# Cross-attention front end: q projected in transposed form, keys stacked four heads at a time

## The reference

```python
def w8a8_linear(x, w, b):                      # int8-like product
    qx, sx = dyn_quant(x)                      # one scale sx per token (row of x)
    qw, sw = quant_weight(w)                   # one scale sw per output channel
    return einsum('bnc,oc->bno', qx, qw) * (sx * sw[:, 0]) + b

q = w8a8_linear(layernorm(x), wq, bq)          # (32, 112, 512), as 16 heads of 32
k = ctx @ wk.T + bk                            # (32, 375, 512)
v = ctx @ wv.T + bv
attn = softmax(q k^T / sqrt(32) + mask)
x1 = x + w8a8_linear(attn v, wo, bo)
out = x1 + mixture_of_experts(layernorm(x1))   # 8 experts, top 2 of them per token
```

## Time and profile before

| | before |
|---|---|
| median of 3 runs | 1605.53 us |
| the profiled execution | 1609.71 us, its span 1608.0 us |
| TensorE busy | 1494.6 us (93%) |
| VectorE, ScalarE, GpSimd busy | 897.5, 884.0, 660.6 us |
| mean granted TensorE clock | 0.965 of full speed |
| DMA, HBM traffic | 281.09 MB moved; 83568 of 220124 packets under 512 B |

### The profile page before, as it was taken

How to read it: one execution, slowest core, us unless ns; L and a number is a source line. 1 busy time by engine, 2 the same in 40 slices (tenths; PEclk the granted TensorE clock), 3 DMA queues, 4 the chain that set the end, 5 groups by cost and what they waited for, 6 DMA issues and landing times. The chain is left out here.

```text
span 1608.0 us, 40123 instructions
## 1 busy us (share of the span) xinstructions
PE 1494.6 (93%) x11594; PEld 1317.6 (82%) x11595; DVE 897.5 (56%) x2365; ACT 884.0 (55%) x2097; POOL 660.6 (41%) x671
## 2 busy tenths in 40 slices
PE   2899999999999999999999999984399999999896
PEld 2788888888888888888888888873299999999895
DVE  6557666766676667666766676654632222222221
ACT  2467667677777776777677767761033333333232
POOL 4233334333443234323432343323555555656453
PEclk9999999999999999999999999985599999999998
DMA  5567777677767776777677767654537776666643
GB/s 173 145 170 196 209 200 197 179 228 205 194 178 226 202 196 179 225 205 196 178 225 201 200 179 222 185 142 141 160 68 186 182 175 134 148 154 125 160 77 48
DMA packets 220124, 281.09 MB, mean 175 GB/s; under 512 B 83568, under 2 KB 164976, under 8 KB 220080
## 3 DMA queue, kind: packets, MB, share of 16 engines
q1 hardware_dynamic: 203952, 247.24, 54.3%
q0 software_dynamic: 16128, 33.30, 11.6%
HBM read 118.31 MB, written 66.17 MB: 115 GB/s over the span
## 5 line engine op out<-in xcount | busy, mean ns | idle before, releaser
L464 DVE CUSTOM_DVE_ANT_0 probs<-score,neg_mask 112x375 f32<-112x375 f32 x512 | 279.7, 546 | 254.8 <-PE score L555 251.5
L392 ACT ACTIVATE probs<-probs,neg_max 112x375 f32<-112x375 f32 x512 | 312.3, 610 | 197.2 <-DVE neg_max L464 191.7
L563 PE MATMUL turn<-ident,probs 112*125 112x112 f32 x1536 | 264.8, 282 | 2.8 <-ACT probs L392 2.5
L385 ACT ACTIVATE probs_t<-turn 125x336 f32<-125x336 f32 x512 | 226.0, 441 | 71.6 <-PE turn L563 70.6
L563 PEld LDWEIGHTS turn<-ident,probs 112*125 112x125 f32 x1536 | 227.2, 190 | 36.4 <-issue 14.4
L555 PE MATMUL score<-k_stack,q_stack 96*112 96x376 f32 x512 | 209.4, 409 | 8.5 <-DMA q_stack<-q_lo 6.2
L591 PE MATMUL proj<-ctx_hi,wk_hi 128*128 128x376 f32 x512 | 176.0, 344 | 1.9 <-PEq L29 1.1
L591 PE MATMUL proj<-ctx_lo,wk_hi 128*128 128x376 f32 x512 | 172.0, 336 | 0.0
L591 PE MATMUL proj<-ctx_hi,wk_lo 128*128 128x376 f32 x512 | 171.7, 335 | 0.0
L1032 DVE TENSOR_TENSOR a_lo<-a_ps,a_hi 128x384 fp32r<-128x384 f32 x63 | 35.1, 557 | 243.7 <-ACT a_hi L1007 243.7
L596 PE MATMUL proj<-wv_hi,ctx_hi 128*125 128x512 f32 x384 | 151.8, 395 | 0.0
(11 more groups left out here) (198 smaller groups left out, 3393.9 us busy)
## 6 DMA issues: line engine op xcount, KB each, us to landing
k_stack<-k_hi SPq DMA_DIRECT2D x512, 94.0 KB, 2.2
k_stack<-k_lo SPq DMA_DIRECT2D x256, 94.0 KB, 2.2
ctx_stage<-ctx_t SPq DMA_DIRECT2D x32, 750.0 KB, 5.0
q_stack<-q_hi SPq DMA_DIRECT2D x256, 56.0 KB, 2.0
w_raw<-gate_up_t SPq DMA_DIRECT2D x32, 352.0 KB, 3.1
gate_up_dram_hi<-w_hi SPq DMA_DIRECT2D x32, 352.0 KB, 4.8
gate_up_dram_lo<-w_raw SPq DMA_DIRECT2D x32, 352.0 KB, 5.2
gate_up_hi<-gate_up_dram_hi SPq DMA_DIRECT2D x16, 704.0 KB, 4.9
```

The costliest lines, as they stand in the source:

```text
L385: act.activation(probs_t[:, h % RING_T, :, :], turn[h % 2][0:LC, 0:LT * N].rearrange("p (l n) -> p l n", l=LT), ACT.Copy).then_inc(turned_ ...
L392: act.activation(probs[:, h % DS, :], probs[:, h % DS, :], ACT.Exp, bias=neg_max[:, par % 2, h:h + 1], scale=-1.0, accum_out=total[:, par ...
L464: dve.tensor_tensor_reduce(probs[:, h % DS, :], score[h % 2][0:N, 0:L], neg_mask[:, p, :], 1.0, BIG, ALU.add, ALU.min, neg_max[:, p, h:h + ...
L563: mm = pe.transpose(turn[h % 2][0:LC, l * N:(l + 1) * N], probs[:, h % DS, l * LC:(l + 1) * LC], W["ident"][0:N, 0:N])
```

## The change

1. Order of channels. The host permutes the output channels of `wq` and `wk` (and both biases) so that head h = 4i + g has its 32 channels on partitions 32i to 32i+31 of group g. The four heads 4i to 4i+3 are then one block of 32 partitions.
2. Keys. `stack_keys(i)` moves four heads by 3 transfers (12 a pass, 24 before), each row contiguous (4 x 376 values). Quarter 3 of the batch is issued at the start of its own pass, quarters 0 to 2 in the pass before. Each needs all four groups of k_lo (before: two), and waits for the scores of the four heads that it overwrites. TensorE waits at heads 0, 4, 8 and 12; ScalarE at h = 3 waits for all four quarters before the first `k_hi` (before: at h = 3 and 7 for one half each).
3. q transposed. At h = 7 sixteen products (bf16, weights 128x128 from `wq_int`, 112 moving columns of `x_int_t`) give q with channels on partitions. The four float32 transposes at h = 9 and their wait for GpSimd go.
4. Scales. The channel scale is now a column, the token scale must be a row: `x_scale` is stored to DRAM at the end of the pass that makes it (112 elements of 4 bytes), fetched as a row spread over 128 partitions in the next pass, and GpSimd multiplies row and column to `q_scale` (128x448), ahead of the bias. VectorE's `q_t` (h = 8) waits for it.
5. q to its place. `q_hi` and `q_lo` (both now from `q_t` in SBUF) are stored together to DRAM by one transfer; SyncE waits until it has landed (`q_kept`), then fetches by 3 transfers. Before: 12 transfers from SBUF to SBUF.
6. SyncE's order: the loads of expert weights stand behind the stores of x1 and h2, x, and the scale row. `q_dram` is issued between quarter 0 and quarter 1 of the keys.
7. `prepare_weights`: no row of channel scales for q (four small activations, eight product records and one copy fewer). VectorE gets 14 semaphore increments ahead of its loop (`LOOP_OFFSET`).

The core of the diff:

```diff
@@ prepare_weights
-            for i, (_, _, row) in enumerate(pairs):
-                act.wait_ge(row_made, i + 1)
-                act.activation(row[0:N, :], ps[0:N, :], ACT.Copy, scale=-inv_sqrt_d if i == 0 else 1.0).then_inc(row_out, 1)
+            act.wait_ge(row_made, 1)
+            act.activation(W["wo_row"][0:N, :], ps[0:N, :], ACT.Copy).then_inc(row_out, 1)
...
+            dve.tensor_scalar(W["wq_col"][:, :], scale[:, 0, :], -inv_sqrt_d, None, ALU.mult).then_inc(bias_done, 1)
@@ attention, SyncE
+            def stack_keys(i):
+
+                rows = slice(QUARTER * i, QUARTER * i + QUARTER)
+                for r, src in ((0, k_hi), (1, k_lo), (2, k_hi)):
+                    sp.dma_start(k_st[QUARTER * r:QUARTER * r + QUARTER, G4 * i:G4 * i + G4, :].bitcast(F32),
+                                 src[rows, :, :].bitcast(F32)).then_inc(k_stacked[i], 16)
...
-                    stack_keys(1)
-                    need(sp, w_stored, 64 * it)
-                    sp.dma_start(w_raw[:, 0:WG], W["gate_up_flat"][:, bass.ds(it * WG, WG)]).then_inc(w_in, 16)
-                    sp.dma_start(w_raw[:, WG:WG + WD], W["down_flat"][:, bass.ds(it * WD, WD)]).then_inc(w_in, 16)
+                    stack_keys(3)
...
                 if has_n:
+                    need(sp, x_scale_stored, 16 * (n + 1))
+                    need(sp, q_scaled, n)
+                    sp.dma_start(x_scale_row[:, :], x_scales[n, :].rearrange("(a t) -> a t", a=1).to_broadcast([128, N])).then_inc(x_scale_in, 16)
+                if has_a:
+                    need(sp, w_stored, 64 * it)
+                    sp.dma_start(w_raw[:, 0:WG], W["gate_up_flat"][:, bass.ds(it * WG, WG)]).then_inc(w_in, 16)
+                    sp.dma_start(w_raw[:, WG:WG + WD], W["down_flat"][:, bass.ds(it * WD, WD)]).then_inc(w_in, 16)
+                if has_n:
                     q = (par + 1) % 2
-                    need(sp, unit_out, UNITS * n + KT // 2)
-                    if has_a:
-                        waited(sp)
-                        need(sp, scored, H * it + H // 2)
-                    stack_keys(0)
-                    need(sp, q_out, 3 * n + 3)
-                    for i in range(4):
-                        rows = slice(QUARTER * i, QUARTER * i + QUARTER)
-                        for r, src in ((0, q_hi), (1, q_hi), (2, q_lo)):
-                            sp.dma_start(q_st[QUARTER * r:QUARTER * r + QUARTER, q, i:H:4, :].bitcast(F32),
-                                         src[rows, :, :].bitcast(F32)).then_inc(q_stacked, 16)
+                    need(sp, unit_out, UNITS * n + KT)
+                    for i in range(3):
+                        if has_a:
+                            waited(sp)
+                            need(sp, scored, H * it + G4 * (i + 1))
+                        stack_keys(i)
+                        if i == 0:
+                            need(sp, q_out, 3 * n + 3)
+                            sp.dma_start(q_dram[n, :, :, :], q_parts[:, :, :, :].bitcast(F32).rearrange("p a g n -> p a (g n)")).then_inc(q_kept, 16)
+                    need(sp, q_kept, 16 * (n + 1))
+                    for r, part in ((0, 0), (1, 0), (2, 1)):
+                        sp.dma_start(q_st[QUARTER * r:QUARTER * r + QUARTER, q, :, :].bitcast(F32).rearrange("p (i g) n -> p i (g n)", g=G4),
+                                     q_dram[n, :, part, :].rearrange("(i p) f -> p i f", p=QUARTER)).then_inc(q_stacked, 16)
...
+                if has_nn:
+                    nn = it + 2
+                    need(sp, ln1, 8 * nn + 5)
+                    with nc.allow_non_contiguous_dma(reason="one scale a token"):
+                        sp.dma_start(x_scales[nn, :].rearrange("(p a) -> p a", a=1), x_scale[:, par % 2:par % 2 + 1]).then_inc(x_scale_stored, 16)
@@ GpSimd
+                    need(pool, x_scale_in, 16 * (n + 1))
+                    need(pool, q_out, 3 * n)
+                    pool.tensor_tensor(q_scale[:, :, :], x_scale_row[:, :].unsqueeze(1).to_broadcast([128, G4, N]),
+                                       W["wq_col"][:, :].unsqueeze(2).to_broadcast([128, G4, N]), ALU.mult).then_inc(q_scaled, 1)
                     need(pool, q_out, 3 * n + 2)
-                    need(pool, q_made, 3 * n)
-                    pool.tensor_tensor(q_tok[:, :], q_tok[:, :], W["bq_row"][0:N, :], ALU.add).then_inc(q_biased, 1)
+                    pool.tensor_tensor(q_t[:, :, :], q_t[:, :, :], W["bq_col"][:, :].unsqueeze(2).to_broadcast([128, G4, N]),
+                                       ALU.add).then_inc(q_biased, 1)
@@ ScalarE
-                        if g % 2 == 0:
-                            need(act, k_stacked[g // 2], 16 * KDMAS * n)
+                        if g == 0:
+                            for i in range(4):
+                                need(act, k_stacked[i], 16 * KDMAS * n)
...
-                        act.activation(q_hi[:, :, :], misc[:, 0:G4 * N].rearrange("p (g n) -> p g n", g=G4),
-                                       ACT.Identity).then_inc(q_hi_made, 1)
+                        need(act, q_biased, n + 1)
+                        need(act, q_kept, 16 * n)
+                        act.activation(q_hi[:, :, :], q_t[:, :, :], ACT.Identity).then_inc(q_hi_made, 1)
@@ VectorE
+                        need(dve, q_scaled, n + 1)
+                        dve.tensor_tensor(q_t[:, :, :], misc[:, 0:G4 * N].rearrange("p (g n) -> p g n", g=G4), q_scale[:, :, :],
+                                          ALU.mult).then_inc(q_out, 1)
...
+                        dve.tensor_tensor(q_lo[:, :, :], q_t[:, :, :], q_hi[:, :, :].bitcast(F32), ALU.subtract).then_inc(q_out, 1)
...
+            for _ in range(LOOP_OFFSET):
+                waited(dve)
@@ TensorE
-                        for t in range(KT):
-                            mm = pe.matmul(misc[0:N, :], x_int_t[:, t, :], W["wq_int"][:, t, :], start=(t == 0), stop=(t == KT - 1))
+                        for g in range(G4):
+                            for t in range(KT):
+                                mm = pe.matmul(misc[:, g * N:(g + 1) * N], W["wq_int"][:, t, 128 * g:128 * g + 128], x_int_t[:, t, :],
+                                               start=(t == 0), stop=(t == KT - 1))
                         mm.then_inc(q_made, 1)
-                    if h == 9 and has_n:
-                        need(pe, q_biased, n + 1)
-                        turn_to_misc(lambda t: q_tok[:, 128 * t:128 * t + 128], W["ident"][0:N, 0:N], misc, N, 128).then_inc(q_made, 1)
```

More of the change, by code:

```diff
@@ L97, in _ @@
             act.wait_ge(ident_made, 3)
-            for i in range(2):
-                act.wait_ge(scale_done, i + 1)
-                for t in range(KT):
-                    act.activation(spread[:, i, t, :], ones[:, :], ACT.Copy, scale=scale[:, i, t:t + 1]).then_inc(spread_done, 1)
+            act.wait_ge(scale_done, 2)
+            for t in range(KT):
+                act.activation(spread[:, t, :], ones[:, :], ACT.Copy, scale=scale[:, 1, t:t + 1]).then_inc(spread_done, 1)
             act.wait_ge(W["ctx_in"], 16)
@@ L128, in _ @@
                                       ALU.subtract).then_inc(ints_done, 1)
-            for i, (_, dst, _) in enumerate(pairs):
+            for i, (_, dst) in enumerate(pairs):
                 for t in range(KT):
@@ L151, in _, with attention @@
                     mm.then_inc(turned, 1)
-                pe.wait_ge(spread_done, KT * (i + 1))
-                if i:
-                    pe.wait_ge(row_out, i)
-                for t in range(KT):
-                    mm = pe.matmul(ps[0:N, 128 * t:128 * t + 128], spread[:, i, t, :], W["ident"][:, :],
-                                   start=True, stop=True)
-                mm.then_inc(row_made, 1)
-def attention(nc, W, x, ctx_t, mask, x1, h2):
+            pe.wait_ge(spread_done, KT)
+            for t in range(KT):
+                mm = pe.matmul(ps[0:N, 128 * t:128 * t + 128], spread[:, t, :], W["ident"][:, :],
+                               start=True, stop=True)
+            mm.then_inc(row_made, 1)
+def attention(nc, W, x, ctx_t, mask, x1, h2, x_scales, q_dram):
     B, N, C = x.shape
@@ L191, in attention @@
         k_st = sb("k_stack", [96, H, LP], F32R)
-        q_hi, q_lo = sb("q_hi", [128, G4, N], F32R), sb("q_lo", [128, G4, N], F32R)
+        q_parts = sb("q_parts", [128, 2, G4, N], F32R)
+        q_hi, q_lo = q_parts[:, 0, :, :], q_parts[:, 1, :, :]
         q_st = sb("q_stack", [96, 2, H, N], F32R)
@@ L203, in attention @@
         x_int, x_int_t = sb("x_int", [N, C], BF16), sb("x_int_t", [128, KT, N], BF16)
-        q_tok = sb("q_tok", [N, C])
+        q_t = sb("q_t", [128, G4, N])
+        x_scale_row, q_scale = sb("x_scale_row", [128, N]), sb("q_scale", [128, G4, N])
         out_ts = sb("out_ts", [128, G4, N])
@@ L224, in attention @@
         unit_made, unit_out = sem("unit_made"), sem("unit_out")
-        k_hi_made, k_stacked = sem("k_hi_made"), [sem("k_stacked0"), sem("k_stacked1")]
```

(12 more changed lines are left out.)

46 lines of the change are left out of this document (20 added, 26 removed).

## The result

The changed kernel takes 1966.92 us (median; 1955.77 to 1972.53) against 1607.07 us before in the same session: a ratio of 1.2222, 95% interval 1.2173 to 1.227. It is slower by 360 us, on the other side of the forecast and outside the range. The profiled execution took 1970.24 us, its span is 1968.5.

What follows compares the result with a forecast made beforehand. TensorE was taken as the bound, SyncE's queue as second nearest its limit. From the profiled 1609.7: - 16.4 - 1.5 - 2.6 + 3.1 = 1592.3, with the runs' median 4.2 lower: 1588 us, range 1577 to 1613.

Steps and rivals of the forecast that it cites:

- What bounds the kernel: Settled passes: TensorE is full, 31.96 of 32 us; SyncE's queue is next, 36 stacking issues taking 23 us.
- rival 1: q's chain through DRAM misses every pass, 0.9 to 1.3 us late before score 0: 1625 us; chance 0.13.
- TensorE's work: Attention passes: four q transposes go, 0.53 us each pass, q product unchanged; 16.4 us less over 31 passes.
- Rival 3: The sixteen q products' weight loads are not hidden on TensorE: 1607 us; chance 0.02.
- prepare_weights: Weight preparation before attention: eight product records for q's scale row go, 1.5 us less, between 0.5 and 1.8.
- Early passes: From 77 to 237 us, TensorE's waits for q go with fewer queue issues: 2.6 us less, bounds 0 and 6.7.
- The first score: End of the pipeline fill: left uncosted, between 1 us gained and 2 lost from q's two DRAM trips.
- The new chain for q: q's store and fetches before score 0: slack 2.3 to -0.2 us, 0.1 us a pass added, 3.1 in all.
- Keys, costed at nothing: Quarter 3, behind weight stores, lands about 617.8 to 618.3, in time for k_hi at 618.33; no cost.
- Rival 4: Late quarter 3 holds up ScalarE's k_hi by 1 us a pass beyond the cover: 1616 us; chance 0.04.
- The scale's store: SyncE's queue ahead of quarter 3: counted in the time of its issues, without a price of its own.
- its sign: Signs of being wrong included score 0 waiting for q_stack every pass and k_hi at h = 3 waiting for k_stack.

Runs made afterwards that it cites:

- h3: Changed kernel, scale row by a TensorE product at h = 2 (no 4-byte store), context, tokens, weight stores behind quarter 3, q's fetches right behind q's store: 1596.77 us.
- g3: Changed kernel, scale row by a TensorE product at h = 5, context, tokens, weight stores behind quarter 3, q by 12 transfers inside SBUF: 1620.17 us.
- e1: Changed kernel without the token scale's 4-byte store, the row fetched from x instead (q scaled by wrong numbers): 1707.88 us, one run.
- i1: h3 with q's three fetches moved back behind keys 1 and 2: 1675.24 us, ratio 1.042.
- e4: Kernel before with the keys' part alone (four heads a transfer, host's channel order), q by 12 transfers, no scale store: 1874.93 us, ratio 1.1667.
- h2: h1 with q's fetches right behind q's store and the scale's store behind the weight stores, directly ahead of its row's fetch: 1838.46 us, ratio 1.1449.
- h1: Whole changed kernel with the scale's store; context, tokens and weight stores behind quarter 3, weights' loads behind x1's tokens: 1711.21 us, ratio 1.064.

## Why the prediction was wrong, by its own steps

**What bounds the kernel** was read rightly: TensorE, then SyncE's queue. The forecast then counted the queue's issues (it takes 13 others a pass, there are 12), and what decided was its bytes between two deadlines. Only rival 1 counted bytes, and those of q's chain alone.

**TensorE's work** came as forecast. The transposes' end took 0.56 us (0.53 said), and the q product did not change. A pass of after, from the score ahead of it to the one behind:

```profile
962.68 0.41 PE L575 MATMUL score<-k_stack,q_stack 96*112 96x376 f32 x1
...
963.44 0.96 PE L659 MATMUL misc<-x_int_t,wq_int 128*128 128x112 bf16 x16
964.24 0.54 PE L583 MATMUL turn<-ident,probs 112*125 112x112 f32 x3
```

Sixteen products take 0.80 us, 0.05 each, against 0.86 for the four of before; the distance of the scores around them is 1.87 in both. Rival 3, weight loads that aren't hidden, is out. No version brings the whole 0.56 to the clock: h3 pays 0.21 for the row's product, and its passes are 32.26 - 31.96 = 0.30 us shorter.

**prepare_weights**: from the second group of transposes to the first projection it is 35.42 - 29.40 = 6.02 us where before had 7.47, so 1.45 (1.5 said). But that group starts 0.92 later, as the first one does (20.04 against 19.12), and 0.5 is left. VectorE has the quantized weight later; which of its new instructions does it was not tried. That 1.45 meets the 1.5 is in part luck: in h3, with the same instructions there, the same distance is 5.37, 2.1 less than before.

**Early passes**: that this time goes once the queue has fewer issues can't be seen in after. h3 comes nearest: its first five passes sum to 158.1 us, those of before to 165.6, and five settled passes differ by 1.5 only. So some 6 go (2.6 said, 6.7 the bound). That the issues alone do it isn't shown: g3, with 24 stacking issues instead of 36, needs 171.0. The first score was left alone, with 2 us lost as the bound; in after it comes at 68.4 us, 9.2 later than before, so 9 of the 360 us arise there (e1, without the store: 63.1).

**The new chain for q** is the second step that failed, and its first rival had the mechanism at half the size. The forecast gave the six key issues 4.4 us (until 636.9, from 632.5); in i1 they take 5.5 (780.39 to 785.91), single ones 1.45, at a DMA share of 0.91 to 1.04. It let the fetches be issued within 1.3 us, they take 2.0, and land 4.4 us after their issue, near the upper end of 4.8. Last, the lateness itself: score 0 of a settled pass stands 3.31 us behind score 15 (median) where h3 has 1.36, so it is 1.95 us late, against 0.9 to 1.3 in the rival, whose 1 us for landing stands on no row. Half clock adds to it in some passes only. Of the 24 waits of 1.55 to 1.86 us between 280 and 1070 us the granted clock fell at 4, and these passes last 35.4 us, the others mostly 33.8; in the pass shown it stayed at full, by the pitch of 0.17 behind score 0. At each of the five earlier waits, 2.1 to 4.2 us long, it fell. All in all the move costs 2.07 us in a settled pass and 2.5 in the mean of all. The rival's 228 GB/s was right in size, 230 and 237 being measured over full shares of 1.02 and 0.99. The Trainium skill, page SBUF — State Buffer, section Door 1: The DMA port swizzle, gives about 218 for 32 partitions; the runs agree within 9%.

**Keys, costed at nothing**, is the step that failed most. It let quarter 3 stand behind 1 MB of weight stores at 362 GB/s and land at 618.3, in time. Its own numbers, put in a row, say otherwise. q's fetches land between 641.3 and 643.8 by its estimate; then context and tokens (1.0 MB, which it left out) and weights (1.08 MB) at 362 need 5.7 us, quarter 3 at 228 another 2.5: 649.5 to 652.0, with ScalarE wanting it at 618.33 + 32.2 - 0.5 = 650.0. That is up to 2 us late before the store is counted, where the text said that 0.5 would still be hidden. It asked of the chain for q what stands ahead of it, and did not ask it of the keys. Rival 4 named the place, ScalarE's k_hi at h = 3, but took 1 us for a lateness that is 6.4 (199.5 / 31).

**The scale's store** got no price at all; it was listed as an issue ahead of quarter 3. It delays what follows by 5 us or so, and since quarter 3 is what follows, all of it fell on the critical path.

**A loop that feeds itself** was not seen. A late k_hi makes a late k_lo, so the window opens later too: nothing is caught up from pass to pass, and the pass becomes as long as window and late work together, 41 us in e4 and 44 in after.

What the forecast named as its sign came true: score 0 waiting for q_stack, and k_hi at h = 3 waiting for k_stack, which it had tied to rivals 1 and 4.

## What to carry to other kernels

When a buffer gets fewer, larger transfers that each read all of it, write down the window from the last write to the next one and sum all bytes of the queue in it, at the rate of the partitions they end in, with everything that is queued between. Add the time to land: here the sums without it were 3 to 4 us short. Moving what has time behind what has none gave 264 us here without touching a byte. Look at a store of single elements by its price and not by its bytes: 448 bytes cost 34 to 259 us in these kernels, depending on what stood behind them.

## What the runs showed of the hardware

- SyncE waited 8.4 us (h2, mean of 32) for a store of 112 elements of 4 bytes to DRAM, 448 bytes in all. In one of these passes it is issued at 821.71 us and has landed at 829.83; the queue still moves 398 GB/s from 822 to 824, 69 until 826, and from there on nothing, at a DMA share of 0.00. With keys behind the store the queue moved 93 and 73 GB/s for eight microseconds (after, h1), where 388 and 380 were reached beside it. In the packet records of after, the key packets of 6016 bytes last 1.1 us on average from 1120 to 1122 us, against 0.42 in e4 (881 to 885 us), and single ones up to 7. Spread 512 bytes apart the same elements cost 15 us in a kernel instead of 34. Why was not tried.
- The Trainium skill, page DMA: Bandwidth & Descriptors, section Specifications, has 512 bytes as the least for the full rate and a read and rewrite below it. No run shows that mechanism. If it were at work here, packed elements would share what is rewritten and spread ones would not, which has the sign of 34 against 15.
- While the DMA share was near 1 (0.91 to 1.04 from 781 to 785 us in i1), SyncE's issue of one key transfer took up to 1.45 us instead of 0.59. That it waits for room in the queue was not tried.
- Waits of the same length are not always followed by half clock: in i1 it came at 4 of 24 waits of 1.55 to 1.86 us. Behind the 7 us waits for a key in after it came in every pass, and the products at half clock make 111 of the 360 us.
